# Self attention of a decoder kernel: one sigmoid, one logarithm, one softplus and the query rotation take other places in their engines' queues

## The chip, the cores and the metric

The kernel runs on one core of a Trainium2 chip. The metric is the time of the device in microseconds (us) for the whole program, a two-layer decoder in one launch. All data are float32.

## The reference, cut to what matters

The program computes six blocks one after the other: self attention, cross attention, an adapter with experts, bucketed attention, latent attention, and a routed feed-forward layer, each with a residual and a layer norm. The change touches the first alone. It works on x of 16 batches, 100 tokens and 256 features:

```python
q = rope((x @ Wq + bq) in 64 heads of 16)            # 4 branches x 16 heads
v = (x @ Wv + bv) in 64 heads of 16
k = rope((x @ Wk + bk) in 16 heads), repeated for the 4 branches
scores = q . k / sqrt(16)
denom = sqrt(clip(sum(k * k), 1e-6))                   # for each key
w = softplus(scores / denom)
w = where(causal, w, 0)
w = w * sigmoid(SCALE * w)                             # SCALE = pi / sqrt(3)
sinks = tanh(sink_scalars) + 1e-6
alpha = 1 / (sum(w) + sinks + 1e-6)
context = (w * alpha) . v + sinks * alpha * v_nulls    # for each of the 64 heads
y = mean over the branches of (context @ Wo + bo)
x = layernorm(x + y)
```

## The kernel before

`self_attention` (line 193) works on one batch at a time in a software pipeline. `four_in_flight` (line 182) calls a `body(o, par)` on each engine 19 times: 4 calls, a hardware loop of two calls to a turn, and 5 calls. In one body four batches are in work: `f = o + 3` is projected (keys, queries), `s = o + 2` gets its scores and weights, `v = o + 1` is multiplied with the values, and `o` is projected, added and normalised. The flags N, F, S, V, O say which of them exist in this body; all do in twelve bodies.

There is no planner. The order of the instructions on each engine is written out by hand in the four `body` functions: TensorE (line 394), VectorE (line 553), ScalarE (line 650), GpSimd (line 754). Each engine does its list in order, and stops at the first `wait_ge` of a semaphore that isn't reached. SyncE only loads weights ahead of the loop.

The steps that the change and the prediction speak of, with the line of the instruction as the profile names it:

- TensorE: `scores` (L346, six parts to a batch, into four banks `pS`), `k_projected` (L293), `q_projected` (L301, two halves), `v_projected` (L313), `values(v, c)` (L368, four parts, into the bank `pb`), `values_turned(v, c)` (L376, transposes `avT` back into `pb`), `k_turned` (L320), `q_turned` (L329), `x_turned` (L286), `context_summed` (L383) and `out_projected` (L390), both in `pb` too.
- VectorE: `masked` (L503, six parts, `pS` to `sm`), `softplus` (L510, three parts: 1152, 1600 and 1600 elements in each partition), `normalised(v, c)` (L523 to L528: the sums of the weights, numerators, reciprocal, product), `kT_read` (L485), `xT_read` (L458), `k_biased` (L464), `k_summed` (L469, L471), `q_biased` (L477), `context_read` (L533), `residual` (L539 to L546), `normed` (L550).
- ScalarE: `sigmoid` (L634, six parts, of the negated scores), `logarithm` (L638, three parts, in place in `L`), `gate` (L642, three parts), `values_read` (L648, `pb` to `avT`), `qT_read` (L627). The three functions sigmoid, logarithm and gate use different activation tables, and each body has three table loads.
- GpSimd: `k_roped` (L701 to L707), `staged` (L691), `k_scaled` (L713, a power of minus one half, and L716), `q_roped(f, 0..3)` (L736 to L748), `rstd` (L723), `residual` (L752).

Softplus is computed as `max(-ln(sigmoid(-s)), s)`: sigmoid and logarithm on ScalarE, the negation and the maximum on VectorE. Part 0 of the logarithm needs the sigmoids of parts 0 and 1 alone (line 637), part 1 those of 2 and 3, part 2 those of 4 and 5. The waits around the change:

```python
    def k_scaled(f):
        po.wait_ge(s_pk, f * 6 + 6)      # key rotated (GpSimd)
        po.wait_ge(s_ks, f + 1)          # square sums (VectorE, k_summed)
    # q_roped(f, 0)
        po.wait_ge(s_qn, 2 * f + 2)      # both halves of the queries biased (VectorE)
    def values(v, b, c):
            pe.wait_ge(s_num, v * 4 + c) # pb read by the sums of part c - 1 (VectorE)
    def values_turned(v, c):
        pe.wait_ge(s_avT, v * 4 + (c + 1))   # copy of the values (ScalarE)
```

Of the kernel before, what the change touches and what calls it, by code (L numbers as in the profile page):

```python
# [192 lines left out]
def self_attention(nc, X, ident, d, later):  # L193
# [13 lines left out]
    with st:  # L207
# [55 lines left out]
        with nc.Block() as block:  # L263
# [188 lines left out]
            def _(dv):  # L452
# [45 lines left out]
                def masked(s, c):  # L498
                    if c == 0:
                        above(dv, s_W, s * NPT)  # L500
                    dv.wait_ge(s_S, s * NCH + (c + 1))
                    n, t, m = (KD * NBR, TB, mask_b) if c < 2 else (NBR, T, mask_a)
                    nc.vector.tensor_tensor(  # L503
                        sm[:, chunk(c)].rearrange("p (e r t) -> p e r t", e=2, t=t),
                        pS[:, 2 * (c % 2):2 * (c % 2) + 2, 0:n * t].rearrange("p e (r t) -> p e r t", t=t),
                        m[:, :].unsqueeze(1).unsqueeze(1).broadcast_to([P, 2, n, t]), ALU.add).then_inc(s_sm, 1)

                def softplus(s, b, n):
                    dv.wait_ge(s_L, s * NPT + (n + 1))
                    nc.vector.scalar_tensor_tensor(out=L[b][:, part(n)], in0=L[b][:, part(n)], scalar=-1.0,  # L510
                                                   in1=sm[:, part(n)], op0=ALU.mult, op1=ALU.max).then_inc(s_W, 1)

                def normalised(v, c):

                    if c == 0:
                        cn.start(v)
                        above(dv, s_cTp, v)
                    dv.wait_ge(s_oNp, v * 4 + (c + 1))
                    o4 = pb[0:T, :].rearrange("p (r h c) -> p r h c", r=2, c=32)
                    n4 = num[:, c // 2, 2 * (c % 2):2 * (c % 2) + 2, :].rearrange("p r (h c) -> p r h c", c=DH)  # L520
                    k3 = csk[:, 2 * HG * c:2 * HG * (c + 1)].rearrange("p (r h) -> p r h", r=2)
                    v4 = csvn[:, 2 * P * c:2 * P * (c + 1)].rearrange("p (r h c) -> p r h c", r=2, c=DH)
                    ins = nc.vector.tensor_tensor(den[:], o4[:, :, :, DH], k3, ALU.add)  # L523
                    nc.vector.tensor_tensor(n4, o4[:, :, :, 0:DH], v4, ALU.add).then_inc(s_num, 1)
                    cn.after(ins)
                    cn.after(nc.vector.reciprocal(alpha[:], den[:]))
                    dv.wait_ge(s_num, v * 4 + (c + 1))
                    nc.vector.tensor_tensor(n4, n4, alpha[:, :, :].unsqueeze(3).broadcast_to([T, 2, HG, DH]), ALU.mult)\  # L528
                        .then_inc(s_nm, 1)
# [23 lines left out]
                def body(o, par):  # L553
                    N, F, S, V, O = parts(o)
                    f, s, v = o + 3, o + 2, o + 1
                    other = (par + 1) % 2
                    if S:
                        masked(s, 0)
                    if F:
                        k_biased(f)  # L560
                    if O:
                        context_read(o)
                    if S:
                        masked(s, 1)
                    if F:
                        q_biased(f, 0)
                    if O:
                        residual(o)
                    if F:
                        q_biased(f, 1)  # L570
                    if S:
                        masked(s, 2)
                    if F:
                        k_summed(f)
                    if S:
                        masked(s, 3)
                    if V:
                        normalised(v, 0)
                    if S:
                        v_biased(s, par, 0)  # L580
                        masked(s, 4)
                    if V:
                        normalised(v, 1)
                    if S:
                        v_biased(s, par, 1)
                        masked(s, 5)
                    if O:
                        normed(o)
                    if V:
                        normalised(v, 2)  # L590
                    if F:
                        kT_read(f, other)
                    if V:
                        normalised(v, 3)
                    if N:
                        xT_read(f + 1, par)
                    if S:
                        softplus(s, par, 0)
                        softplus(s, par, 1)
                        softplus(s, par, 2)  # L600

# [20 lines left out]
            @block.scalar  # L622
            def _(ac):
                def qT_read(f, b):
                    ac.wait_ge(s_qTp, f + 1)
                    above(ac, s_S, (f - 1) * NCH)
                    nc.scalar.copy(qT[b][:, :, :, :].rearrange("p k r t -> p k (r t)"), pq[:, :, 0:NBR * T])\  # L627
                        .then_inc(s_qT, 1)

                def sigmoid(s, b, c):  # L630
                    ac.wait_ge(s_sm, s * NCH + (c + 1))
                    if c == 0:
                        above(ac, s_av, (s - 1) * 4)
                    nc.scalar.activation(L[b][:, chunk(c)], sm[:, chunk(c)], ACT.Sigmoid, scale=-1.0).then_inc(s_E, 1)  # L634

                def logarithm(s, b, n):
                    ac.wait_ge(s_E, s * NCH + 2 * (n + 1))
                    nc.scalar.activation(L[b][:, part(n)], L[b][:, part(n)], ACT.Ln, bias=tiny[:, 0:1]).then_inc(s_L, 1)  # L638

                def gate(v, b, n):  # L640
                    ac.wait_ge(s_W, v * NPT + (n + 1))
                    nc.scalar.activation(L[b][:, part(n)], L[b][:, part(n)], ACT.Silu, scale=CS).then_inc(s_G, 1)  # L642

                def values_read(v, c):
                    n = v * 4 + c
                    ac.wait_ge(s_av, n + 1)
                    above(ac, s_oNp, n)
                    nc.scalar.copy(avT[:, :, :].rearrange("p q t -> p (q t)"), pb[:, 0:4 * T]).then_inc(s_avT, 1)  # L648

                def body(o, par):  # L650
                    N, F, S, V, O = parts(o)
                    f, s, v = o + 3, o + 2, o + 1
                    other = (par + 1) % 2
                    if V:
                        for n in range(NPT):
                            gate(v, other, n)
                    if S:
                        sigmoid(s, par, 0)
                    if V:
                        values_read(v, 0)  # L660
                    if S:
                        sigmoid(s, par, 1)
                        sigmoid(s, par, 2)
                    if V:
                        values_read(v, 1)
                    if S:
                        sigmoid(s, par, 3)
                    if V:
                        values_read(v, 2)
                    if S:  # L670
                        sigmoid(s, par, 4)
                    if V:
                        values_read(v, 3)
                    if S:
                        sigmoid(s, par, 5)
                    if F:
                        qT_read(f, other)
                    if S:
                        logarithm(s, par, 0)
                        logarithm(s, par, 1)  # L680
                        logarithm(s, par, 2)

                ac.wait_ge(s_w, 16 * NW)
                nc.scalar.activation(sink[:], sink[:], ACT.Tanh).then_inc(s_c, 1)
                four_in_flight(ac, body)

            @block.gpsimd
            def _(po):
# [65 lines left out]
                def body(o, par):  # L754
                    N, F, S, V, O = parts(o)
                    f, s, v = o + 3, o + 2, o + 1
                    if F:
                        k_roped(f)
                    if N:
                        staged(f + 1)  # L760
                    if F:
                        k_scaled(f)
                        q_roped(f, 0)
                        q_roped(f, 1)
                    if O:
                        rstd(o)
                    if V:
                        residual(v)
                    if F:
                        q_roped(f, 2)  # L770
                        q_roped(f, 3)
# [2034 lines left out]
```

## Time and profile before

| | |
|---|---|
| median of 3 runs | 2555.2 us (2553.42 to 2560.78) |
| profiled execution | 2563.16 us |
| its span | 2561.5 us |
| mean granted clock of TensorE | 0.912 |
| TensorE matmuls busy | 2135.1 us (83% of the span) |
| VectorE busy | 1355.6 us (53%) |
| ScalarE busy | 1128.6 us (44%) |
| GpSimd busy | 474.4 us (19%) |
| end of self attention | 588.93 us of the span |

The first block, self attention, takes the time from about 40 us to 589 us of the span. Busy time is the time in which an engine has an instruction running; a wait is idle time ahead of an instruction, put down to what released it. The granted clock is a share of TensorE's full speed: 1.0 is 2.4 GHz, 0.5 is 1.2 GHz. Times in a timeline are counted from the start of the span.

### The profile page before, as it was taken

The numbers are of one execution on the slowest core, as the hardware profiler recorded it, in microseconds if no ns is written. First come the engines' busy times: TensorE is split into PE (matmuls) and PEld (weight loads), VectorE is DVE, ScalarE is ACT, GpSimd is POOL, SyncE is SP. The second block draws the span as 40 slices with busy tenths as digits, with TensorE's granted clock in tenths as the row PEclk, the third lists the DMA queues.
The fourth block names the chain that finished last, engine by engine and source line by source line (L and its number), as shares of the span: only waits on it lengthen the run. The fifth ranks groups of instructions, "written<-read, shape, count | busy, mean of one in ns | idle before, by whom it ended". The sixth has DMA issues, their size and how long they took to land. (4 is left out here: it accounts for less than half of the span.)

```text
span 2561.5 us, 48525 instructions
## 1 busy us (share of the span) xinstructions
PE 2135.1 (83%) x17362; PEld 1314.8 (51%) x17363; DVE 1355.6 (53%) x3264; ACT 1128.6 (44%) x2404; POOL 474.4 (19%) x533
## 2 busy tenths in 40 slices
PE   1888888864999999777777999999999999963992
PEld 0454555442666665554443555655555555552661
DVE  1577777751455555358883455555555555432223
ACT  0566666650555555135552444444444444420110
POOL 2455555510000000224440000000000000003002
PEclk9789999975999999779997999999999999966996
DMA  5000000006000000000000000000000000026101
GB/s 153 1 2 1 0 0 0 2 1 185 19 18 12 17 15 2 1 1 0 0 0 18 7 7 6 6 6 12 6 6 6 6 6 7 1 78 223 33 31 58
DMA packets 50461, 60.83 MB, mean 24 GB/s; under 512 B 9849, under 2 KB 44974, under 8 KB 49918
## 3 DMA queue, kind: packets, MB, share of 16 engines
q1 hardware_dynamic: 47366, 53.74, 6.8%
q0 software_dynamic: 3008, 5.91, 0.8%
q8 instruction: 57, 0.93, 0.2%
q14 instruction: 30, 0.25, 0.0%
HBM read 51.11 MB, written 8.52 MB: 23 GB/s over the span
## 5 line engine op out<-in xcount | busy, mean ns | idle before, releaser
L2155 DVE CUSTOM_DVE_ANT_0 la_pr<-la_pS,la_mb 100x461 f32<-100x461 f32 x256 | 148.1, 636 | 197.2 <-PE la_pS L2018 197.2
L2000 PE MATMUL la_side<-la_wkv,la_inT 128*128 128x512 f32 (+1 forms) x512 | 243.4, 598 | 0.0
L2256 ACT ACTIVATE la_pr<-la_pr,la_nm 100x461 f32<-100x461 f32 x256 | 171.9, 674 | 135.8 <-DVE la_nm L2155 135.8
L1988 PE MATMUL la_side<-la_inT,la_wkv 128*128 128x461 f32 x512 | 227.2, 566 | 0.8 <-ACT la_inT L2240 0.8
L2264 ACT COPY la_pT<-la_pPT 128x400 f32<-128x400 f32 x256 | 126.2, 493 | 165.4 <-PE la_pPT L2026 164.1
L2026 PEld LDWEIGHTS la_pPT<-io_ident,la_pr 100*128 100x128 f32 x1024 | 110.4, 144 | 149.0 <-issue 105.7
L1028 DVE TENSOR_REDUCE ca_nm<-ca_pS 100x2 f32<-100x722 f32 x128 | 116.2, 908 | 112.5 <-PE ca_pS L915 110.6
L2323 POOL TENSOR_TENSOR la_xb<-io_X,la_bo 100x256 f32<-100x256 f32 x16 | 11.6, 728 | 840.4 <-DVE io_X L2144 840.4
L2026 PE MATMUL la_pPT<-io_ident,la_pr 100*128 100x100 f32 x1024 | 137.5, 257 | 29.7 <-ACT la_pT L2264 18.4
L1100 ACT ACTIVATE ca_pr<-ca_pS,ca_nm 100x361 f32<-100x361 f32 x256 | 130.0, 561 | 64.4 <-DVE ca_nm L1028 62.6
L2117 DVE COPY la_v<-la_side 128x512 f32<-128x512 f32 (+1 forms) x128 | 87.8, 686 | 101.3 <-PE la_side L2000 101.2
L1988 PEld LDWEIGHTS la_side<-la_inT,la_wkv 128*128 128x128 f32 x512 | 89.3, 191 | 87.8 <-issue 86.2
L2000 PEld LDWEIGHTS la_side<-la_wkv,la_inT 128*128 128x128 f32 (+1 forms) x512 | 86.5, 180 | 86.8 <-issue 86.4
L2244 ACT COPY la_kT<-la_side 128x461 f32<-128x461 f32 x128 | 68.5, 536 | 128.8 <-PE la_side L1988 128.8
L2018 PE MATMUL la_pS<-la_kT,la_qT 64*100 64x461 f32 x512 | 116.5, 573 | 0.0
L915 PE MATMUL ca_pS<-ca_kT,ca_qTm 32*100 32x361 f32 x512 | 111.2, 510 | 0.3
L2165 DVE TENSOR_SCALAR la_pr<-la_pr,la_zs 100x461 f32<-100x461 f32 x256 | 106.4, 458 | 4.5
L648 ACT COPY sa_avT<-sa_pb 128x400 f32<-128x400 f32 x64 | 31.5, 492 | 172.3 <-PE sa_pb L368 172.3
L2036 PE MATMUL la_pav<-la_pT,la_v 128*64 128x100 f32 x2048 | 106.9, 259 | 0.4
L368 PEld LDWEIGHTS sa_pb<-sa_L,sa_va 64*32 64x32 f32 x4096 | 71.1, 111 | 58.5 <-issue 58.5
L2036 PEld LDWEIGHTS la_pav<-la_pT,la_v 128*64 128x64 f32 x2048 | 94.1, 142 | 9.1 <-issue 2.1
L1759 ACT ACTIVATE ba_pr<-ba_A,ba_mx 100x100 f32<-100x100 f32 x256 | 75.8, 369 | 48.1 <-DVE ba_mx L1707 46.2
(356 smaller groups left out, 4372.7 us busy)
## 6 DMA issues: line engine op xcount, KB each, us to landing
rf_w<-in_L_ffn_W SPq DMA_DIRECT2D x16, 1024.0 KB, 14.0
ca_cn<-in_ctx SPq DMA_DIRECT2D x16, 256.0 KB
la_cn<-in_ctx SPq DMA_DIRECT2D x16, 256.0 KB, 2.7
rows_in<-io_zero SPq DMA_DIRECT2D x20, 128.0 KB, 4.6
rb_xr<-rows_in POOLq DMA_DIRECT2D x20, 128.0 KB, 2.3
rows_out<-rb_yr SPq DMA_DIRECT2D x20, 128.0 KB, 1.7
ea_wcT<-in_t_L_ffn_conv_W SPq DMA_DIRECT2D x1, 2048.0 KB
la_wkv<-in_L_xattn_Wkv SPq DMA_DIRECT2D x1, 2048.0 KB
```

Of the source, the lines that this page charges most:

```text
L915: last = nc.tensor.matmul(pS[0:T, 2 * (m % 2) + e, 0:SC], qTm[b][rows_, h // HG, h % 2, :], kT[b][rows_, h // HG, :], start=True, stop=True)
L1028: nc.vector.reduce_max(nm[m % 2][:], pS[0:T, 2 * (m % 2):2 * (m % 2) + 2, 0:SC], AX, negate=True)\
L1100: ins = nc.scalar.activation(pr[m % NP][:, e, 0:SC], pS[0:T, 2 * (m % 2) + e, 0:SC], ACT.Exp, bias=nm[m % 2][:, e:e + 1])
L1988: last = nc.tensor.matmul(pf[:, 0:SK], wkv[:, k, e * P:(e + 1) * P], inT[:, k, :], start=k == 0, stop=k == KD - 1)
L2000: last = nc.tensor.matmul(pf[0:keys[c], :], inT[:, k, c * P:c * P + keys[c]], wkv[:, k, o:o + 512], start=k == 0, stop=k == KD - 1)
L2018: last = nc.tensor.matmul(o[e], qT[b][half[e], m, :], kT[b][half[e], m, :], start=True, stop=True)
L2026: last = nc.tensor.transpose(pPT[:, c * T:(c + 1) * T], pr[m % 2][:, e, c * P:(c + 1) * P], ident[0:T, 0:T])
L2036: last = nc.tensor.matmul(pav[DX * e:DX * (e + 1), m % 4, :], v[b][:, c, (2 * m + e) * DX:(2 * m + e + 1) * DX], pT[m % 2][:, e, c * T:(c ...
L2155: ins = nc.vector.tensor_tensor_reduce(out=pr[m % 2][:, e, 0:SK], in0=pS[0:T, 2 * (m % 2) + e, 0:SK], in1=mb[b][:, :], scale=-1.0, scalar= ...
L2165: ins = nc.vector.tensor_scalar(pr[m % 2][:, e, 0:SK], pr[m % 2][:, e, 0:SK], zs[m % 2][:, 2 + e:3 + e], None, ALU.mult)
L2256: ins = nc.scalar.activation(pr[m % 2][:, e, 0:SK], pr[m % 2][:, e, 0:SK], ACT.Exp, scale=-1.0, bias=nm[m % 2][:, e:e + 1], accum_out=zs[m ...
L2264: nc.scalar.copy(pT[m % 2][:, e, :], pPT[:, 0:NC * T]).then_inc(s_PT, 1)
```

## The change

Three of the four `body` functions get another order. Nothing is added or taken out.

- VectorE: `normalised(v, 2)` goes ahead of `normed(o)`; `softplus(s, par, 0)` goes ahead of `normalised(v, 3)` and `xT_read`.
- ScalarE: `sigmoid(s, par, 5)` and `logarithm(s, par, 0)` go ahead of `values_read(v, 3)` and `qT_read`.
- GpSimd: `q_roped(f, 0)` goes ahead of `k_scaled(f)`.

```diff
--- before.py
+++ after.py
@@ -584,18 +584,19 @@
                     if S:
                         v_biased(s, par, 1)
                         masked(s, 5)
+                    if V:
+                        normalised(v, 2)
                     if O:
                         normed(o)
-                    if V:
-                        normalised(v, 2)
                     if F:
                         kT_read(f, other)
+                    if S:
+                        softplus(s, par, 0)
                     if V:
                         normalised(v, 3)
                     if N:
                         xT_read(f + 1, par)
                     if S:
-                        softplus(s, par, 0)
                         softplus(s, par, 1)
                         softplus(s, par, 2)
@@ -669,14 +670,14 @@
                         values_read(v, 2)
                     if S:
                         sigmoid(s, par, 4)
+                    if S:
+                        sigmoid(s, par, 5)
+                        logarithm(s, par, 0)
                     if V:
                         values_read(v, 3)
-                    if S:
-                        sigmoid(s, par, 5)
                     if F:
                         qT_read(f, other)
                     if S:
-                        logarithm(s, par, 0)
                         logarithm(s, par, 1)
                         logarithm(s, par, 2)
@@ -759,8 +760,8 @@
                     if N:
                         staged(f + 1)
                     if F:
+                        q_roped(f, 0)
                         k_scaled(f)
-                        q_roped(f, 0)
                         q_roped(f, 1)
                     if O:
                         rstd(o)
```

## Rows read from the trace of the kernel before

**Rows 1.** Busy time by stretch: length, then busy us (instructions) of each engine, clock, DMA.
```profile
118.85:518.39 399.54, 340.06 (x4732) 205.95 (x4733) 284.37 (x546) 251.19 (x261) 210.14 (x233) 0.93 0.00 1
365.39:395.41 30.02, 27.14 (x364) 17.17 (x365) 21.84 (x42) 19.30 (x21) 16.19 (x18) 0.89 0.00 0
90.73:104.72 13.99, 13.36 (x43) 6.93 (x43) 8.33 (x9) 12.28 (x10) 2.57 (x6) 0.57 0.01 2
```

**Rows 2.** Waits of TensorE, 118.85 to 518.39 us: total, times, longest.
```profile
PE sa_pb L390 <- DVE sa_cxT L533: 26.6, 13, 2.7
PE sa_pb L368 <- DVE sa_num L524: 15.3, 13, 1.2
PE sa_pq L329 <- POOL sa_qr L748: 12.2, 13, 1.0
```

**Rows 3.** Timeline of TensorE, one body: start, duration, instruction, [idle before <- releaser].
```profile
376.92 1.11 PE L390 MATMUL sa_pb<-sa_wo,sa_cxT 128*100 128x256 f32 x4 [0.72 <-DVE sa_cxT L533]
...
379.68 0.94 PE L346 MATMUL sa_pS<-sa_qT,sa_kTm 32*128 32x400 f32 x4
...
393.28 1.15 PE L368 MATMUL sa_pb<-sa_L,sa_va 64*32 64x100 f32 x64 [1.17 <-DVE sa_num L524]
395.41 0.90 PE L329 MATMUL sa_pq<-io_ident,sa_qr 100*128 100x100 f32 x8 [0.98 <-POOL sa_qr L748]
396.15 0.60 PE L376 MATMUL sa_pb<-io_ident,sa_avT 128*100 128x128 f32 x4
...
397.43 0.76 PE L346 MATMUL sa_pS<-sa_qT,sa_kTm 32*128 32x144 f32 x8 [0.51 <-ACT sa_qT L627]
...
406.40 1.92 PE L390 MATMUL sa_pb<-sa_wo,sa_cxT 128*100 128x256 f32 x4 [2.71 <-DVE sa_cxT L533]
```

**Rows 4.** Timeline of ScalarE, the same body.
```profile
394.87 0.87 ACT L634 ACTIVATE sa_L<-sa_sm 128x800 f32<-128x800 f32 x1
396.35 0.83 ACT L627 COPY sa_qT<-sa_pq 128x800 f32<-128x800 f32 x1 [0.60 <-PE sa_pq L329]
397.19 1.28 ACT L638 ACT_TABLE_LOAD   x1
398.49 4.30 ACT L638 ACTIVATE sa_L<-sa_L,sa_tiny 128x1152 f32<-128x1152 f32 x3
```

**Rows 5.** Timeline of VectorE, the same body.
```profile
379.78 0.69 DVE L477 TENSOR_TENSOR sa_qn<-sa_pq,sa_bq 100x512 f32<-100x512 f32 x1 [0.42 <-PE sa_pq L301]
...
391.40 0.99 DVE L503 TENSOR_TENSOR sa_sm<-sa_pS,sa_mask_a 128x800 f32<-128x800 f32 x1 [0.69 <-PE sa_pS L346]
...
392.71 0.41 DVE L524 TENSOR_TENSOR sa_num<-sa_pb,sa_csvn 100x256 f32<-100x256 f32 x1
...
397.83 0.36 DVE L458 COPY sa_xT<-sa_pk 128x200 f32<-128x200 f32 x1
399.77 1.36 DVE L510 SCALAR_TENSOR_TENSOR sa_L<-sa_L,sa_sm 128x1152 f32<-128x1152 f32 x1 [1.59 <-ACT sa_L L638]
401.30 3.56 DVE L510 SCALAR_TENSOR_TENSOR sa_L<-sa_L,sa_sm 128x1600 f32<-128x1600 f32 x2 [0.16 <-ACT sa_L L638]
```

**Rows 6.** Timeline of GpSimd, the same body.
```profile
382.36 2.92 POOL L713 TENSOR_TENSOR sa_kf<-sa_kss,sa_half 100x16 f32<-100x16 f32 x1 [2.10 <-DVE sa_kss L471]
...
385.93 1.29 POOL L736 TENSOR_TENSOR sa_qa<-sa_qn,sa_cos 100x512 f32<-100x512 f32 x1
...
393.95 1.33 POOL L748 TENSOR_TENSOR sa_qr<-sa_qa,sa_qb 100x512 f32<-100x512 f32 x1
```

**Rows 7.** Timelines of three engines in the first bodies and in the first of the last.
```profile
76.67 0.69 DVE L477 TENSOR_TENSOR sa_qn<-sa_pq,sa_bq 100x512 f32<-100x512 f32 x1 [1.69 <-PE sa_pq L301]
...
79.25 2.92 POOL L713 TENSOR_TENSOR sa_kf<-sa_kss,sa_half 100x16 f32<-100x16 f32 x1 [5.80 <-DVE sa_kss L471]
...
118.85 0.91 PE L329 MATMUL sa_pq<-io_ident,sa_qr 100*128 100x100 f32 x8 [0.57 <-POOL sa_qr L748]
...
528.96 2.03 PE L390 MATMUL sa_pb<-sa_wo,sa_cxT 128*100 128x256 f32 x4 [5.29 <-DVE sa_cxT L533]
```

## The prediction, made before the change was run

> **What bounds the kernel now.** I read the granted clock and busy time of the self-attention stage first, then what TensorE waited for in it, then one body of its loop in order of time on each engine. The change touches nothing outside this stage, and the stage ends in a barrier with the weight loads of the next stage behind it, so a microsecond won here should be one at the end.
>
> From the turning of the queries in one body to that in the 13th body after it the stage takes 399.54 us, 30.73 us for a body, at a mean granted clock of 0.93 [rows 1]. That clock says how much is lost to its lower level: 0.07 x 30.73 = 2.15 us a body. One kind of body (9 of the 13) falls to half speed at the output projection, right behind a wait of 2.71 us; the other kind (4 of the 13, as the second row of [rows 1], clock 0.89) falls among the transposes, loses 3.3 us by 0.11 x 30.02, and then hardly waits there. TensorE's named waits are 26.6 us for the projected context's copy, 15.3 for the third sums (the buffer `pb` behind `values(3)`) and 12.2 for the rotated queries [rows 2]; with some 3 us for the queries' copy that is 57 us, 4.4 a body.
>
> The full-speed work of a body follows from one undisturbed turn [rows 3]: 376.92 to 379.68 is 2.76; 379.68 to 393.28 less the wait of 1.17 is 12.43; 393.28 to 406.40 less 0.98, 0.51 and 2.71 is 8.92. Together 24.1, and 24.1 + 4.4 + 2.15 = 30.65, which meets the measured 30.73. So TensorE is the engine to look at, and its waits are what can be won. The wait of 2.71 is the end of one chain: last sigmoid, the queries' copy, a table load, three logarithms (ScalarE), three softplus (VectorE, in order), mask, key bias, copy of the context, output projection [rows 4, 5].
>
> **The change part by part**, in the clock times of the body of [rows 3 to 6]. No arithmetic is added or removed; the instructions and DMAs are the same, only places in four queues change, and no DMA or queue of SyncE is passed.
>
> 1. Sums before `normed`. The third sums start where the last mask ends, 391.40 + 0.99 = 392.39, instead of 392.71 [rows 5]. `values(3)` starts at 392.96 instead of 393.28: its wait is 0.85 instead of 1.17. `normed` comes 0.8 later and only the next body's `rstd` needs it: nothing.
>
> 2. Query rotation before key factors. GpSimd idled 2.10 us until the square sums and began the factors at 382.36 [rows 6]; the queries' bias was done at 379.78 + 0.69 = 380.47 [rows 5]. With the two products (1.29 us each, [rows 6]) in that hole, everything behind comes 1.8 earlier, because the work is the same: rotated queries at 395.28 - 1.8 = 393.5. The keys are scaled about 0.8 later, near 386.8, and their turning is at 391.8 and waits in TensorE's order: covered, with 5 us to spare. Query turning then waits only for `values(3)`, 392.96 + 1.15 = 394.1 instead of 395.41. Wait of 0.98 gone. The third multiply of the sums now meets the last rotation on GpSimd; its cost is bounded by 0 and the 0.5 until that ends, and the key copy behind it is not needed before 397: I take nothing.
>
> 3. Last sigmoid and first logarithm before the last copy of the values. The sigmoid needs the last mask: 392.45 to 393.32; table load 1.28 [rows 4]: 394.6; first logarithm 1.25 (start of the logarithms 398.49, first softplus released at 399.77): 395.9. Only now comes the copy of the values, 395.9 to 396.4, which stood 1.4 earlier before (ahead of the sigmoid at 394.87). This is what the change pays: TensorE, done with the queries at 394.85, waits for it about 1.5 us. Then the queries' copy, 0.83, to 397.1, against 397.18 before: first scores at 397.25 instead of 397.43. The other two logarithms, 4.30 - 1.25 = 3.05, end at 400.15 instead of 402.79.
>
> 4. First softplus before the last sums. 395.9 to 397.3 on VectorE, in the time in which it waited for TensorE. The last turning of values (0.60 long) ends at 397.0, so the sums begin 0.2 behind it; sums and the copy of x took 1.4 from there (396.75 to 397.83 + 0.36), so x is ready at 398.6 and the key projection waits 0.7 that it did not wait before. From the first scores on TensorE then has 406.40 - 2.71 - 397.43 = 6.26 of work to the output projection: 397.25 + 0.7 + 6.26 = 404.2. The other chain: two softplus from 398.7, 3.56 long [rows 5], to 402.3 (404.86 before); from there to the output projection it was 1.55, so the copy is there at 403.8. The two meet within 0.4 us, and the 2.71 is gone.
>
> New waits: 0.85 + 1.5 + 0.05 + 0.7 = 3.1. A body at full clock: 24.1 + 3.1 = 27.2. Behind 406 the gates, the mask and the projections follow 2.2 earlier with TensorE as the last to arrive everywhere: between 379.68 and 391.77 it waited for nobody.
>
> 5. The clock. Not shown by the trace of before; bounds 0 and 2.15 us a body. The stretch behind the 2.71 us wait loses its cause; the one among the transposes keeps it, with 3.1 us of waits within 6 us where there were 2.7 (1.17, 0.98, 0.51). I take 1.3, somewhat over half. Body: 28.5.
>
> 6. Ahead and behind. In the body before the first value product the factors began at 79.25 and the queries' bias ended at 77.36: rotation 1.8 earlier, where TensorE stood waiting for it. The next turning, which waited 0.57 for GpSimd [rows 7], gains that and the 0.3 of point 1, 0.9. The very first body is left at nothing. Behind the last turned queries the output projection waited 5.29 [rows 7]; it came 10.57 after the turning, now 403.8 - 394.1 less the copy of x that is not there, 9.35: 1.2; the following body has the same chain, 1.3, and 0.3 by point 1. Together 1.8 + 0.9 + 2.8 = 5.5 (bounds 2 and 8).
>
> Sum: 13 x (30.73 - 28.5) = 29.0, and 5.5: **34.5 us**. The profiled execution took 2563.16 us (its span 2561.5), 8 us over the median of 2555.2; it would become 2528.7, the median **2521**.
>
> **Weighed against the skill.** The trace shows table loads of 1.28 us with the activation right behind (397.19 + 1.28 = 398.47, start 398.49) [rows 4], and the copy of the queries just ahead of a load, under the sigmoid's table. The new order has copies between two logarithms. The Trainium skill (ScalarE: Activation LUTs, "Table sets: the hidden batching unit") says that cheap functions such as copy are in every set, so no load should be added; no row of this stage shows a copy under the logarithm's table. The same page ("What ACT_TABLE_LOAD costs") prices a switch at about 2.66 us, a drain being added; the rows show no drain. By that price two added switches would cost 5.3 us a body, and as an estimate from the page the change would be a loss of some 35 us; it rests on a load that the page itself does not expect.
>
> **The rivals.**
> A. The waits go, the clock takes its share: the half-speed stretch among the transposes comes in every body, 2.15 us lost as now. For it: the waits sit closer together than before. Against: it came in only 4 of 13. Body 29.35, gain 18 + 5.5 = 23.5: 2532.
> B. The clock stays at full speed: 13 x 3.53 + 5.5 = 51: 2504. For it: no wait over 1.5 us is left. Against: [rows 1], the second row.
> C. Copies between logarithms take two table loads more, 2.57 us on ScalarE. The copy of the context then comes at 403.8 + 2.57 = 406.4, where it was before: nothing won in a body, and 5 at the ends: 2550.
> D. Slower: the waits of 1.5 and 0.7 throw the clock to half speed until the values of the next body begin. The place is the 14 us behind the query turning in the body at 90.73, granted 0.57 [rows 1], behind a long wait: 0.43 x 14 = 6.0 lost, of which the 0.7 hides: body 32.5, 13 x 1.8 - 5.5 = 18 more: 2573. It decides from a clock loss of 30.73 - 27.2 = 3.5 us a body on. Against: after waits of up to 2.71 the stretches here cost no more than 3.3.
>
> **How the numbers follow.** Forecast 0.58, A 0.20, B 0.10, C 0.07, D 0.05. The range leaves out C and D and most of what lies under B: 2503 to 2543. This kernel's runs differ by some 0.3%, 7.7 us, so faster by more than that takes forecast, A and B and a little of C: 0.89; within it 0.06, slower 0.05.
>
> **What would show it.** Right: in the stage, the wait of the output projection for the context's copy at 0 to 0.3 us where it was 2.71; the wait of the query turning for GpSimd gone; a new wait of about 1.5 us in front of the last turning of values, for the copy of ScalarE, and 0.7 before the key projection; the factors on GpSimd behind two products, its idle time of 2.1 there gone; bodies of 27.2 to 29.4 us. Wrong: more than 16 loads for the logarithm (C), a clock under 0.88 over the 13 bodies (D), an output projection that still waits over 1 us (the chain of logarithms and softplus was not shortened by 2.6), or later stages that change by more than 3 us.

## The result, and the profile after

The changed kernel takes 2528.7 us at the median (4 runs, 2523.0 to 2533.0) against 2557.8 for the kernel before in the same comparison: ratio 0.9895, interval 0.9877 to 0.9913, by the ratio some 27 us faster (22 to 31), by the medians 29. Forecast were 34.5 us and 2521; rival A had 23.5 and 2532. The measured gain lies between the two.

The profiled executions are 40.1 us of span apart (2561.5 and 2521.4), more than the medians, since before's (2563.2) was slower than each of its four timed runs and this one (2523.0) is the fastest of its four. Of the 40.1, the last output projection of the block comes 37.1 earlier (584.37 before, 547.31 after); 3.0 lie behind the block, where nothing was changed; no run explains them.

Stretches of the changed kernel (columns as in [rows 1]): the same 13 bodies, then one long and one short body (a body counted from one query turning to the next).

```profile
114.81:486.00 371.19, 334.75 (x4741) 206.65 (x4733) 281.07 (x545) 249.41 (x261) 208.71 (x233) 0.93 0.00 1
...
280.63:311.84 31.21, 28.66 (x373) 17.88 (x364) 21.83 (x43) 19.18 (x21) 16.09 (x18) 0.84 0.00 0
311.84:338.75 26.91, 23.96 (x373) 14.65 (x365) 21.58 (x44) 19.19 (x21) 16.07 (x18) 1.00 0.00 0
```

The mean body is 371.19 / 13 = 28.55 us, 30.73 before [rows 1]. But no body has this length: eight take 26.9 at clock 1.00 and five 31.2 at 0.84. What TensorE waited for in the 13 bodies (as [rows 2]):

```profile
PE sa_pb L376 <- ACT sa_avT L649: 17.6, 13, 1.4
PE sa_pb L368 <- DVE sa_num L524: 11.0, 13, 0.8
PE sa_pk L293 <- DVE sa_xT L458: 6.6, 12, 0.8
```

The waits for the context's copy and for the rotated queries [rows 2] are gone. The 1.35 us for the copy of the values and most of the wait for the copy of x (up to 0.8) are new. In order of time, a short body on TensorE:

```profile
310.76 1.15 PE L368 MATMUL sa_pb<-sa_L,sa_va 64*32 64x100 f32 x64 [0.85 <-DVE sa_num L524]
311.84 0.91 PE L329 MATMUL sa_pq<-io_ident,sa_qr 100*128 100x100 f32 x8
314.11 0.64 PE L376 MATMUL sa_pb<-io_ident,sa_avT 128*100 128x128 f32 x4 [1.35 <-ACT sa_avT L649]
...
316.43 1.11 PE L293 MATMUL sa_pk<-sa_wk,sa_xT 128*100 128x256 f32 x4 [0.60 <-DVE sa_xT L458]
...
321.71 1.03 PE L390 MATMUL sa_pb<-sa_wo,sa_cxT 128*100 128x256 f32 x4
```

Lay this beside [rows 3]: from the third values to the output projection it takes 10.95 us (310.76 to 321.71) where it took 13.12 (393.28 to 406.40). The 1.35 comes from ScalarE, where sigmoid, load and logarithm now stand ahead of the copy. No table load is added (16 for the logarithm in the block, before and after); the copies run between the logarithms:

```profile
310.24 0.87 ACT L635 ACTIVATE sa_L<-sa_sm 128x800 f32<-128x800 f32 x1 [0.61 <-DVE sa_sm L503]
311.12 1.28 ACT L639 ACT_TABLE_LOAD   x1
312.42 1.25 ACT L639 ACTIVATE sa_L<-sa_L,sa_tiny 128x1152 f32<-128x1152 f32 x1
313.58 0.47 ACT L649 COPY sa_avT<-sa_pb 128x400 f32<-128x400 f32 x1
313.95 0.84 ACT L628 COPY sa_qT<-sa_pq 128x800 f32<-128x800 f32 x1
314.67 3.16 ACT L639 ACTIVATE sa_L<-sa_L,sa_tiny 128x1600 f32<-128x1600 f32 x2
```

A long body has the same waits of 0.85 and 1.35, but behind them TensorE runs at half speed. Its first scores already take 1.16 us in place of 0.76, so the clock has fallen ahead of the third wait, which shrinks to 0.25. The 16 context matmuls take 3.57 us, 1.93 in a short body:

```profile
282.90 0.65 PE L376 MATMUL sa_pb<-io_ident,sa_avT 128*100 128x128 f32 x4 [1.35 <-ACT sa_avT L649]
283.38 0.34 PE L286 MATMUL sa_pk<-io_ident,sa_xs 100*128 100x100 f32 x2
283.81 1.16 PE L346 MATMUL sa_pS<-sa_qT,sa_kTm 32*128 32x144 f32 x8
285.22 2.03 PE L293 MATMUL sa_pk<-sa_wk,sa_xT 128*100 128x256 f32 x4 [0.25 <-DVE sa_xT L458]
287.04 3.57 PE L383 MATMUL sa_pb<-io_ident,sa_num 100*128 100x100 f32 x16
290.54 1.33 PE L346 MATMUL sa_pS<-sa_qT,sa_kTm 32*128 32x144 f32 x8
```

The granted clock in this stretch, and at its end, where it rises again:

```profile
285.20:291.80 6.60, 6.58 (x28) 5.63 (x28) 4.95 (x5) 6.57 (x5) 1.81 (x4) 0.50 0.00 0
291.80:294.80 3.00, 3.00 (x6) 1.16 (x5) 0.76 (x1) 2.11 (x3) 1.69 (x5) 0.59 0.00 0
294.80:297.00 2.20, 2.20 (x9) 1.17 (x7) 1.72 (x5) 0.00 (x0) 0.00 (x0) 1.00 0.00 0
```

### The profile page after: what moved, and what is told of

It reads as the page before. It is cut to its first block and busy times, and to the rows that moved or that the text cites. A ratio compares the mean times of both kernels' runs of the same rounds, so it can differ in the third digit from the quotient of the medians.

```text
span 2521.4 us, 48525 instructions
## 1 busy us (share of the span) xinstructions
PE 2123.3 (84%) x17362; PEld 1312.1 (52%) x17363; DVE 1353.3 (54%) x3264; ACT 1126.2 (45%) x2404; POOL 473.7 (19%) x533
## 5 line engine op out<-in xcount | busy, mean ns | idle before, releaser
L2027 PE MATMUL la_pPT<-io_ident,la_pr 100*128 100x100 f32 x1024 | 137.6, 258 | 29.7 <-ACT la_pT L2265 18.4
L649 ACT COPY sa_avT<-sa_pb 128x400 f32<-128x400 f32 x64 | 31.2, 487 | 145.1 <-PE sa_pb L368 145.1
```

Of the source, the lines that this page charges most:

```text
L2027: last = nc.tensor.transpose(pPT[:, c * T:(c + 1) * T], pr[m % 2][:, e, c * P:(c + 1) * P], ident[0:T, 0:T])
```

## The experiments

"Short body" is an undisturbed one, with the clock at 1.00 throughout (in `gpsimd_only` there is one, the first of the 13; for before it is the turn of [rows 3]); "13 bodies" is from the third to the last query turning (L329), in the profiled execution. The experiments came in three comparisons with before medians of 2554.4, 2556.4 and 2558.6 us.

| kernel | median, us | ratio to before (interval) | 13 bodies | clock there | short body |
|---|---|---|---|---|---|
| before | | | 399.5 | 0.93 | 29.5 (worked out) |
| changed | 2528.7 | 0.9895 (0.9877 to 0.9913) | 371.2 | 0.93 | 26.9 |
| `after_again` | 2530.6 | 0.9898 (0.9883 to 0.9912) | 381.6 | 0.90 | 26.9 |
| `gpsimd_only` | 2554.8 | 0.9995 (0.9980 to 1.0011) | 398.6 | 0.92 | 29.6 |
| `gpsimd_and_sums` | 2539.7 | 0.9928 (0.9913 to 0.9943) | 383.0 | 0.96 | 28.4 |
| `no_gpsimd` | 2545.9 | 0.9962 (0.9949 to 0.9975) | 384.5 | 0.89 | 26.9 |
| `normed_back` | 2522.5 | 0.9862 (0.9842 to 0.9882) | 372.1 | 0.92 | none, 26.9 worked out |
| `softplus_back` | 2531.8 | 0.9907 (0.9886 to 0.9928) | 375.8 | 0.94 | 27.7 |
| `scalar_back` | 2600.2 | 1.0166 (1.0143 to 1.0189) | 444.6 | 0.85 | none |
| `before_spare` | 2540.7 | 0.9928 (0.9914 to 0.9942) | 382.8 | 1.00 | 29.5 |
| `spare_matmuls` | 2500.8 | 0.9777 (0.9765 to 0.9790) | 349.8 | 1.00 | 26.9 |
| `x_and_context_first` | 2508.2 | 0.9826 (0.9801 to 0.9851) | 353.2 | 0.96 | 26.2 |
| `x_context_spare` | 2489.7 | 0.9743 (0.9730 to 0.9755) | 340.2 | 1.00 | 26.2 |

**GpSimd's part alone**, on the kernel before.

```diff
+                        q_roped(f, 0)
                         k_scaled(f)
-                        q_roped(f, 0)
```

> The kernel before with only GpSimd's part of the change (query rotation ahead of the key factors). Theory (one chain from the last mask over sigmoid, logarithm and softplus to the output projection): the turning of queries comes some 1.0 us earlier, but the queries' copy and the logarithms behind it follow by only 0.7 to 0.8, because the last sigmoid still stands in front of them; wait of the output projection stays near 2.7, body 30.0 at the mean instead of 30.7, 9 us in the 13 bodies and 3 at the start, total 12 us faster than before. Rival (the rotated queries were what held TensorE, the other moves only shift waits): 20 us or more faster, output projection's wait under 1.5 us.

Nothing was won, a miss of the theory by its 12 us and of the rival too. The query turning waits for nobody, but the third values now wait 2.09 us where they waited 1.17. VectorE and GpSimd at that place:

```profile
140.91 1.33 DVE L550 TENSOR_SCALAR io_X<-sa_y,sa_mv,sa_rs 100x256 f32<-100x256 f32 x1
```
```profile
140.82 1.26 POOL L748 TENSOR_TENSOR sa_qr<-sa_qa,sa_qb 100x512 f32<-100x512 f32 x1
```

`normed`, 0.40 us before, stands still until the last rotation ends at 142.1 and keeps the third sums waiting behind it. The Trainium skill (SBUF — State Buffer, "Who interferes with whom") says that VectorE in a 2-port mode, which `tensor_scalar` can enter, and GpSimd shut each other out of their shared ports for a whole instruction. The rows agree in the time, 1.33 against 0.40, ending with the rotation; that ports are the reason no run shows.

**That, tested**: the same with the third sums ahead of `normed`.

```diff
+                    if V:
+                        normalised(v, 2)
                     if O:
                         normed(o)
```

> The kernel before with the query rotation ahead of the key factors and the third sums ahead of normed; the logarithms and softplus stay. Theory (in the run with GpSimd's part alone, normed, 1.33 us instead of 0.40, was held up by the last query rotation, and the third sums stood behind it): the wait of the third values falls from 2.09 to 0.85 us, the query turning waits for nobody, and the queries' copy comes 0.7 to 0.8 earlier; undisturbed body 28.7 instead of 29.5, 10 us faster in the 13 bodies, 14 in all. Rival (the rotation moves nothing, whatever stands around it): 0 to 4 us, as with GpSimd's part alone.

19 us (15 to 22), short body 28.4 (28.7 expected): the wait of the third values fell to 11.0 us in 13 times, 0.85 each, and `normed` takes 0.40 again. So the held-up `normed` ahead of the sums was what ate the gain. The gain is above the 14: the body is 0.3 shorter than expected, and the clock over the 13 bodies is 0.96.

**The changed kernel with `normed` back** ahead of the third sums.

```diff
-                    if V:
-                        normalised(v, 2)
                     if O:
                         normed(o)
+                    if V:
+                        normalised(v, 2)
```

> The changed kernel with normed ahead of the third sums again. Theory (slack by the copy of the values): normed collides with the last rotation and takes 1.33 us, the third values wait 2.1 us instead of 0.85, but TensorE's wait of 1.35 for the copy of the values shrinks by the same, so the undisturbed body is 26.9 to 27.1 us. In all within 5 us of the changed kernel, apart from the number of bodies with a half-speed stretch. Rival (what holds up the third sums holds up the body): undisturbed body 28.1, 15 us slower.

The third values wait 27.2 us in 13 times, 2.1 each, and TensorE's wait for the copy of the values is gone but for one. It costs the whole nothing: the median is 6 to 8 us below the changed kernel's, in a comparison of its own. The bodies are 27.4, 27.8 and 30.1 long in turn at clocks 0.98, 0.95 and 0.84, so none is undisturbed. But the middle one runs at full speed up to its last value product:

```profile
259.33 0.91 PE L329 MATMUL sa_pq<-io_ident,sa_qr 100*128 100x100 f32 x8
...
285.15 2.04 PE L368 MATMUL sa_pb<-sa_L,sa_va 64*32 64x100 f32 x64 [2.09 <-DVE sa_num L524]
```

From 259.33 to 285.15 are 25.82 us, in the short body of the changed kernel that begins at 311.84 as well:

```profile
337.66 1.15 PE L368 MATMUL sa_pb<-sa_L,sa_va 64*32 64x100 f32 x64 [0.85 <-DVE sa_num L524]
```

The undisturbed body is 26.9, as expected. What the clock takes is about the same as well, 372.1 - 13 x 26.9 = 22.4 us in the 13 bodies. So the move of `normed`, needed with the rotation alone, is not needed with the rest.

**Without GpSimd's part.**

```diff
-                        q_roped(f, 0)
                         k_scaled(f)
+                        q_roped(f, 0)
```

> The changed kernel with GpSimd's order of before. Theory: TensorE waits for the rotated queries again (0.98 us), but the wait for the copy of the values behind it shrinks by as much (1.35 to 0.1), so the undisturbed body stays 26.9 to 27.1 us, and only the start loses 3 to 4 us: within 5 us of the changed kernel, 24 to 30 faster than before. Rival (the parts add up): it loses the 12 us that the part alone brings, undisturbed body 27.7.

The short body is 26.9, so the parts don't add up, as expected:

```profile
204.10 1.15 PE L368 MATMUL sa_pb<-sa_L,sa_va 64*32 64x100 f32 x64 [0.85 <-DVE sa_num L524]
206.44 0.90 PE L329 MATMUL sa_pq<-io_ident,sa_qr 100*128 100x100 f32 x8 [1.18 <-POOL sa_qr L749]
207.45 0.64 PE L376 MATMUL sa_pb<-io_ident,sa_avT 128*100 128x128 f32 x4
```

The wait moves from the values' copy to the queries. But the gain over before is 10 us (6 to 13), not 24 to 30: the first bodies end 4.4 us later than in the changed kernel (119.20 against 114.81; 3 to 4 expected), and eight of the 13 have a half-speed stretch, clock 0.89. The profiled execution is the fastest of its eight, so the others have lost more. Order alone did not decide this one.

**Softplus back**, behind the last sums and the copy of x.

```diff
-                    if S:
-                        softplus(s, par, 0)
...
                     if S:
+                        softplus(s, par, 0)
                         softplus(s, par, 1)
```

> The changed kernel with the first softplus back behind the last sums and the copy of x (first logarithm still early). Theory: the wait of the key projection (0.6 us) goes, and the output projection waits for the context's copy again, about 1.5 us, because all three softplus stand in a row behind the copy of x; undisturbed body 27.7 instead of 26.9, 10 us slower than the changed kernel. Rival (the early logarithm is what counts, VectorE has room): no difference, body 26.9.

Short body 27.7, as expected, though the waits that make it are not: the key projection keeps 0.42 us of its wait, which was to go, and the output projection waits 0.78 us, where 1.5 were expected.

```profile
209.00 1.11 PE L293 MATMUL sa_pk<-sa_wk,sa_xT 128*100 128x256 f32 x4 [0.42 <-DVE sa_xT L458]
...
215.23 1.11 PE L390 MATMUL sa_pb<-sa_wo,sa_cxT 128*100 128x256 f32 x4 [0.78 <-DVE sa_cxT L533]
```

The total is nearly the changed kernel's all the same, some 3 us slower by the ratios and not 10: four bodies over 31 us and one of 28.4, the clock 0.94. Most of what order lost, the clock gave back.

**ScalarE's order back.** The first softplus stays ahead of the last sums.

```diff
-                    if S:
-                        sigmoid(s, par, 5)
-                        logarithm(s, par, 0)
                     if V:
                         values_read(v, 3)
+                    if S:
+                        sigmoid(s, par, 5)
                     if F:
                         qT_read(f, other)
                     if S:
+                        logarithm(s, par, 0)
```

> The changed kernel with ScalarE's order of before: the first softplus now stands ahead of the last sums, but its logarithm comes as late as before. Theory: sums, copy of x, key projection and context all wait for the late logarithm, a wait of about 3.5 us ahead of the key projection; undisturbed body about 29.8, as long as before or 0.3 longer: 0 to 10 us slower than the kernel before. Rival (VectorE's order alone brings the gain): 10 us or more faster than before.

42 us slower than before, where 0 to 10 were expected. The wait ahead of the key projection is there (56.6 us in 13), and the clock falls behind it in every body, which I had not reckoned: 34.1 us each.

```profile
398.18 2.03 PE L293 MATMUL sa_pk<-sa_wk,sa_xT 128*100 128x256 f32 x4 [4.32 <-DVE sa_xT L458]
400.00 3.57 PE L383 MATMUL sa_pb<-io_ident,sa_num 100*128 100x100 f32 x16
```

The body as a stretch, with its clock of 0.85:

```profile
390.00:424.10 34.10, 28.11 (x380) 17.56 (x371) 21.76 (x43) 19.18 (x20) 16.05 (x19) 0.85 0.00 0
```

From the key projection to the output projection it takes 9.68 us here (398.18 to 407.86) and 5.28 at full speed (316.43 to 321.71 above), 4.4 less, so 29.7 remain, the 29.8 that were expected. VectorE's part of the change without ScalarE's is worse than nothing.

**The clock by itself.** The changed kernel again, and with matmuls in its waits that nobody reads:

```diff
+                def spare(s, n):
+                    above(pe, s_sm, (s + 1) * NCH)
+                    for _ in range(n):
+                        nc.tensor.matmul(pS[:, 2, UA:512], wo[:, 0, 0:P], wq[:, 0, 0:512 - UA], start=True, stop=True)
...
+                    if S and F:
+                        spare(s - 1, 3)
                     if F:
                         k_projected(f, other)
...
                     if F:
                         q_turned(f)
+                    if S and F:
+                        spare(s, 6)
```

> The changed kernel once more, for comparison on one chip with the next three. Theory: 29 us faster than before (ratio 0.989), bodies of two kinds again: 26.9 us at clock 1.0, and 31.2 at 0.84 with a half-speed stretch of 10 us from the first scores to the query projection; 4 to 7 of 13 are long, and that number makes the spread of the runs.

> The changed kernel; TensorE does 6 matmuls of 128x112 whose result nobody reads behind the query turning (about 1.2 us, in the wait of 1.35) and 3 ahead of the key projection (0.6 us, in the wait of 0.6). Theory (the waits among the transposes bring the clock down): all bodies 26.9 to 27.3 us at clock 1.0, mean 27.1 instead of 28.6, 19 us faster than the changed kernel. Rival 1 (the clock falls whatever TensorE does there): body kinds as before, 0 to 5 us slower. Rival 2 (the added work delays): undisturbed body 27.5 or more.

The repeat has seven long bodies in place of five, 10.4 us more in the 13, and its profiled execution is 9.3 us longer in all: so much of this kernel's spread is the number of long bodies. With the spare matmuls all 13 bodies are 26.9:

```profile
116.17:466.00 349.83, 337.60 (x4975) 217.56 (x4967) 279.80 (x545) 249.43 (x261) 208.72 (x233) 1.00 0.00 1
```
```profile
304.56 0.91 PE L329 MATMUL sa_pq<-io_ident,sa_qr 100*128 100x100 f32 x8
305.30 1.51 PE L397 MATMUL sa_pS<-sa_wq,sa_wo 128*128 128x112 f32 x12
306.82 0.65 PE L376 MATMUL sa_pb<-io_ident,sa_avT 128*100 128x128 f32 x4
```

More work in TensorE's queue, and 30 us faster than the changed kernel in the same comparison (19 were expected, with fewer long bodies reckoned). The idle time in these waits is what brings the clock down; that it falls whatever TensorE does there is refuted, and nothing is delayed. Which of the two fillings is needed was not tested apart.

**The same in the kernel before.**

```diff
+                    if F and O:
+                        spare(pq[:, 1, UA:512], 12)
                     if O:
                         out_projected(o)
...
+                    if S and F:
+                        above(pe, s_sm, (s + 1) * NCH)
+                        spare(pS[:, 2, UA:512], 4)
                     if F:
                         q_turned(f)
```

> The kernel before, with 12 matmuls of 128x112 that nobody reads ahead of the output projection (2.4 us, in the wait of 2.71) and 4 ahead of the query turning (0.8 us, in the wait of 0.98). Theory (the waits bring the clock down, and the change wins 2.6 us of order in each body beside it): all 13 bodies 29.5 to 29.7 us at clock 1.0, 14 to 17 us faster than before; the difference to the changed kernel with its spare matmuls, both at full clock, stays 13 x 2.6 = 34 us. Rival (most of what the changed kernel won is clock): within 10 us of the changed kernel with spare matmuls.

All 13 bodies take 29.3 to 29.5, clock 1.00, and the whole is 18 us faster than before (14 to 17 expected):

```profile
120.54:503.36 382.82, 359.80 (x5151) 238.56 (x5149) 283.81 (x546) 251.03 (x261) 210.24 (x233) 1.00 0.00 1
```

So the parts separate: by order alone, both at full clock, the change brings 382.8 - 349.8 = 33.0 us in the 13 bodies. The clock cost the kernel before 399.5 - 382.8 = 16.7 and costs the changed one 21.4 (371.2) to 31.7 (381.6).

Body by body, before's nine bodies of 31.1 us lose 1.7 to the clock, and its four of 29.8 to 30.0, with the stretch among the transposes, only 0.4: there the output projection's wait of 2.71 shrank to 0.72 [rows 3] and took up most of the stretch. The changed kernel has no such wait left, and a long body loses 31.2 - 26.9 = 4.3.

**Three more moves**: x turned on TensorE ahead of the last values and read ahead of the last sums, the context copied between the second and third softplus (it leaves its place ahead of `masked(s, 1)` in the next body). The second kernel has `spare(s, 4)` ahead of `x_turned` too. VectorE's part:

```diff
                     if S:
                         softplus(s, par, 0)
+                    if N:
+                        xT_read(f + 1, par)
                     if V:
                         normalised(v, 3)
-                    if N:
-                        xT_read(f + 1, par)
                     if S:
                         softplus(s, par, 1)
+                    if V:
+                        context_read(v)
+                    if S:
                         softplus(s, par, 2)
```

> The changed kernel with three more moves: x is turned on TensorE ahead of the last values and read on VectorE ahead of the last sums, and the context is copied between the second and third softplus. Theory: the wait of 0.6 us ahead of the key projection and 0.4 of the one of 1.35 go; undisturbed body 26.3, 8 us faster than the changed kernel, if the share of long bodies stays. Rival (VectorE is the bound and gates and masks come later for it): 0 to 5 us slower than the changed kernel, with a wait of the values or of the second scores in place of it.

> The kernel with the three moves, and 4 matmuls of 128x112 whose result nobody reads ahead of the turning of x (0.8 us, in the wait for the copy of the values). Theory: clock 1.0 in all bodies, body 26.3 to 26.6, 25 us faster than the changed kernel. Rival: the clock still falls in some bodies, since 0.8 us of work is too little; between 0 and 10 faster.

Nine bodies of 25.8 to 26.7 (mean 26.2, 26.3 expected), four of 27.8 to 30.8, and 22 us faster than the changed kernel where 8 were expected: again the clock (0.96). The wait for the copy of the values is 8.1 us in the 13 bodies where it was 17.6; that this is why the clock falls less often is likely, not shown. With four spare matmuls the clock holds in all 13, and this is the fastest kernel: 2489.7 us, 66 us under before and 41 under the change (25 expected).

## Why the prediction was right, and where it was off

The four parts of the order did what the forecast says of each, and the body held: 28.55 us in the profiled execution, 28.5 forecast. That the number fits so well is luck in part: the order brought more than was forecast and the clock took more, and in the repeat the body is 29.35, which is rival A's.

1. *Sums before `normed`.* Wait 0.85, as forecast. The reason given was too small: the 0.3 us of `normed`. Together with the early rotation `normed` would take 1.33, and without the late copy of the values behind it that costs the body 1.2 us (29.6 in `gpsimd_only` against 28.4 in `gpsimd_and_sums`).
2. *Rotation first.* The query turning waits for nobody; the last rotation ends 1.8 earlier. The third multiply of the sums, for which I took nothing, takes 0.79 us where it took 0.83. Unforeseen: the lower bound on the square sums (L471) now takes 1.13 us where it took 0.17, until a rotation product ends; the factors start 0.2 behind the products, and nothing on the path is late.

```profile
299.62 1.30 POOL L738 TENSOR_TENSOR sa_qb<-sa_qn,sa_sin 100x512 f32<-100x512 f32 x1
```
```profile
299.82 1.13 DVE L471 TENSOR_SCALAR sa_kss<-sa_kss 100x16 f32<-100x16 f32 x1
```

3. *Sigmoid and logarithm first.* New wait 1.35 (forecast 1.5).
4. *Softplus first.* Key projection waits 0.60 (0.7); the output projection's 2.71 is gone.
   The short body is 26.9 (27.2 forecast).
5. *Clock.* This is the term that was mis-sized. It took 1.65 us a body in the profiled execution (28.55 - 26.9) and 2.4 in the repeat, against 1.3 taken and 2.15 as upper bound. The bound was worked out from the mean clock, which counts the whole of a half-speed stretch as lost. Before lost only 16.7 / 13 = 1.3, because part of its stretches ran in time that is otherwise a wait. So the bound was too high for before, and yet too low for the changed kernel, where a stretch among the transposes has no long wait behind it: by 0.16 x 31.2 it loses 5.0 us by the mean clock, 4.3 of them in length, where before it lost 3.3 and 0.4. I took it that the order wins its waits and the clock gives some back beside it; in fact the wait of 2.71 had been hiding clock loss. And the stretch comes in five to seven of 13 bodies, not in the four of before.
   The order brought 33.0 at full clock. The forecast's own undisturbed bodies, 24.1 and the waits of [rows 3] (5.37), 29.5, and 27.2 after, give 13 x 2.3 = 30. The two errors partly cancel.
6. *Ahead and behind.* 4.0 (118.85 to 114.81) against 2.7, and 4.7 behind the last query turning (65.98 to 61.31) against 2.8. Together 8.7, 0.7 over the upper bound that I gave for the ends. Of my signs of being wrong one is at its limit: the later stages differ by 3.0 us (over 3), though in a profiled execution of before slower than all its timed runs. The others are not met. Of the bodies, 27.2 to 29.4 us, only the mean lies in the range.

Rival C (two table loads) is refuted by the rows of ScalarE, and so what the Trainium skill says, that copy is in every set (ScalarE: Activation LUTs, "Table sets: the hidden batching unit"), holds for the logarithm's too. The Trainium skill's price for a switch (the same page, "What ACT_TABLE_LOAD costs"), with a drain, is not what these rows show: the load starts 0.01 us behind the sigmoid and the logarithm 0.02 us behind the load. Rival D did not come in the changed kernel, but its mechanism did in `scalar_back`: a wait of 4.3 us and a half-speed stretch in all 13 bodies.

Left open: why the stretch comes in 5 bodies of one run and 7 of another of the same kernel, and why it lasts some 10 us there and some 7 in before (0.11 x 30.02, doubled for the half speed).

## What to carry to other kernels

In a hand-ordered pipeline follow the one chain that ends each body, and move its instructions ahead of everything that others can wait for, on all engines at once: undoing ScalarE's part alone cost some 70 us against the whole. Then look at where the remaining waits of TensorE lie, and what stands behind them: a half-speed stretch costs little ahead of a wait that it can use up (0.4 us a body before) and nearly all that it slows down where none is left (4.3 after). Here two short waits, 0.85 and 1.35 us, were enough to bring one on, and cheap matmuls in the waits gave back 30 us. To judge an order by itself, compare both kernels with the clock held.

## What the runs showed of the hardware

- In 5 of 13 bodies of the changed kernel (7 of 13 in the repeat) TensorE's clock fell from 2.4 to 1.2 GHz behind waits of 0.85 and 1.35 us, with value products and transposes between and after them, for some 10 us of half-speed work; with 1.5 and 0.8 us of matmuls of 128x112 in the waits of 1.35 and 0.6 it stayed at 1.00 through 350 us.
- A `tensor_scalar` of VectorE from SBUF to SBUF in float32 is held up by GpSimd's `tensor_tensor`: 1.33 us instead of 0.40 (100x256) and 1.13 instead of 0.17 (100x16). A VectorE product of two SBUF inputs took 0.79 to 0.83 beside a rotation product. The power on GpSimd (L713, in the changed kernel L714) did not hold it up: the same product took 0.43 us under it.

```profile
301.12 2.92 POOL L714 TENSOR_TENSOR sa_kf<-sa_kss,sa_half 100x16 f32<-100x16 f32 x1 [0.20 <-issue]
```
```profile
302.45 0.43 DVE L528 TENSOR_TENSOR sa_num<-sa_num,sa_alpha 100x256 f32<-100x256 f32 x1
310.81 0.79 DVE L528 TENSOR_TENSOR sa_num<-sa_num,sa_alpha 100x256 f32<-100x256 f32 x1
```

- A 128x112 float32 matmul of the spare kind takes 1.51 / 6 = 0.25 us in a row of six.
- Copies of ScalarE between two logarithms needed no table load of their own (16 loads for the logarithm before and after), and a load of 1.28 us had no more than 0.02 us of idle time on either side.
